# A macaron block on one core: GpSimd multiplies the quantised h by its block scales instead of VectorE, with the order lists rewritten

## The chip, the cores and the metric

The kernel runs on one core of one Trainium2 chip. The metric is the device time of one execution in microseconds (us), smaller is better; the time before is the median of three runs.

## The reference

For 32 sequences of 512 tokens with 256 features the reference computes three residual layers one after the other:

```
x = x + 0.5 * ffn(layernorm(x))        # called A below
x = x + attn(layernorm(x))             # called S: a selective state-space scan, 16 states
x = x + 0.5 * ffn(layernorm(x))        # called C, same weights as A

ffn(x):  gate = q(x) @ q(w_gate).T ; y = q(x) @ q(w_up).T ; h = silu(gate) * y ; return q(h) @ q(w_down).T
q(v):    in blocks of 16: scale = max|v| / 6 ; v / scale rounded to the grid {0, .5, 1, 1.5, 2, 3, 4, 6} ; times scale
attn:    h_t = exp(A dt) h_(t-1) + (...) x_t   for each feature and each of 16 states; y = sum_n h C_n + D x
```

h has 704 features, so each token has 44 blocks of 16, each with a scale.

## The kernel before

All data of a sequence lies with 128 tokens on the partitions, so a sequence has four token tiles (T = 4). An ffn pass quantises x, transposes it, multiplies by the gate and up weights in eight half-tile steps, quantises h tile by tile, transposes h and multiplies by the down weights. The scan has 16 states by 2 halves of the features: 32 steps of 128 x 512.

The engines run a software pipeline. One body of the loop handles one sequence in each of the stages: A (first ffn, pass q = 2 it - 2), S (scan of the sequence before), C (second ffn of the one before that) and N (norm and quantisation of x for the next A). Within a body each engine works through its own list, written out by hand in `ORDER`, strictly in that order; the engines are held together by semaphores alone. 29 bodies use the full lists, and the bodies at either end use the same lists with the stages that exist there. Each piece of a list is a stage, a step and a number. The steps that matter here, with the line of the profile for what they issue:

- ffn, VectorE: `hid` (L717, silu times up, half a tile), `am` (L722, block maxima of a tile of h), `qs` (L728 to L733, scales and their reciprocals for two tiles), `qm` (L737, a maximum with a constant, bf16), `qp` (L743, grid value times block scale into `qh`), `res` (L748, the residual), `xa`, `xs`, `xv`, `xm`, `qy` (L665 to L706, the same quantisation for x), `ln` (L649 to L658).
- ffn, GpSimd: `mv` (L456, h times reciprocal), `mh` (L464 and L471, add and subtract a magic number, which leaves the grid value in `grid`), `mx` (L443, L447, the same for x).
- ffn, ScalarE: `gu` (L939, silu), `ah` and `ax` (L930, L926, absolute value), `ht` (L920, copies transposed h out of PSUM), `tx` (L910).
- ffn, TensorE: `gu` (L1120), `ht` (L1101, transposes `qh`; three to a tile), `dn` (L1127), `tx` (L1082).
- scan, VectorE: `tb`, `cb`, `sc` (L757 to L774), `k` (L786), `dt` (L779, L781), `g` (L793, the scan of one step), `p` (L803, its product with C), `y` (L812).
- scan, GpSimd: `xl` (L426), `bl` (L437). ScalarE: `xh`, `b` (L989), `z` (softplus, L960 to L972), `d` (L999, one decay; exponential). TensorE: `z` (L1160), `k` (L1168), `w` (L1186, the input of one scan step), `c` (L1196), `e` and `p` (L1206).

A scan step m is tied to its neighbours: `g` waits for `w` and `d` of the same m; `w` waits for `g` of m - 2, since it writes the same half of `w_ps`; `w` also needs `b` and `bl` of its state.

## Time and profile before

| what | value |
|---|---|
| time, median of 3 runs (lowest to highest) | 4114.31 us (4113.19 to 4118.74) |
| the profiled execution: time, and its span | 4118.5 us, 4116.8 us |
| mean granted clock of TensorE | 0.970 |
| one body of the steady loop | 122.05 us |

The span runs from the first to the last instruction of the profiled execution. "Busy" is the time in which an engine has an instruction in it. TensorE's ends are modelled, so its busy share is not a share of its peak. The steady bodies repeat each other closely, so one of them (from 2010.2 to 2132.25 us, and its successor) stands for all.

### The profile page before, as it was taken

To read this page: it belongs to the slowest core of one execution; us is meant where nothing else is said; L and a number is where in the kernel's file an instruction comes from. 1 tells how busy PE (TensorE), PEld (TensorE's weight loads), DVE (VectorE), ACT (ScalarE), POOL (GpSimd) and SP (SyncE) were. 2 spreads that over 40 slices of the span, in tenths; PEclk is the share of its full clock that TensorE was granted. 3 is DMA by queue.
4 is the path that set the end of the run, shared out by engine and by line. 5 is a ranking of instruction groups with operands and counts; after the bars stand their busy time and mean duration, and the time that the engine had idled before them with its cause. 6 is when DMAs were issued, how large, how long until landed. Compare 5 with 4: busy or idle time off the path is not lost. (4 is left out here: it accounts for less than half of the span.)

```text
span 4116.8 us, 81697 instructions
## 1 busy us (share of the span) xinstructions
PE 3662.4 (89%) x29740; PEld 2754.3 (67%) x29740; DVE 3740.5 (91%) x6358; ACT 3191.1 (78%) x6115; POOL 2154.0 (52%) x1779
## 2 busy tenths in 40 slices
PE   1689999999999999999999999999999999999986
PEld 0367766667766666776666776666777666677664
DVE  6489999999999999999999999999999999999985
ACT  1368888778888777888877888877788887788863
POOL 1345555555655555555555565555555555556533
PEclk9799999999999999999999999999999999999988
DMA  1000000000000000000000000000000000000000
GB/s 28 11 11 17 7 13 15 17 16 17 6 17 12 17 16 17 17 6 12 16 16 17 17 7 17 11 17 16 17 17 6 12 16 17 17 17 6 11 11 11
DMA packets 46452, 57.93 MB, mean 14 GB/s; under 512 B 7463, under 2 KB 41704, under 8 KB 46056
## 3 DMA queue, kind: packets, MB, share of 16 engines
q1 hardware_dynamic: 46056, 52.72, 3.8%
q8 instruction: 240, 3.93, 0.4%
q14 instruction: 156, 1.28, 0.1%
HBM read 19.16 MB, written 16.78 MB: 9 GB/s over the span
## 5 line engine op out<-in xcount | busy, mean ns | idle before, releaser
L793 DVE TENSOR_TENSOR_SCAN state<-w_ps,decay 128x512 f32<-128x512 f32 x1024 | 1212.9, 1213 | 13.3 <-ACT decay L999 9.2
L1120 PE MATMUL gu_ps<-wgu,qxT 128*128 128x352 f16 x6144 | 1037.0, 319 | 116.7 <-DVE hid L717 78.8
L1120 PEld LDWEIGHTS gu_ps<-wgu,qxT 128*128 128x128 f16 x6144 | 572.6, 99 | 513.1 <-DVE hid L717 126.9
L1186 PE MATMUL w_ps<-bdif,x_parts 128*128 128x129 f16 (+1 forms) x12288 | 866.5, 224 | 46.4 <-DVE state L793 22.8
L1186 PEld LDWEIGHTS w_ps<-bdif,x_parts 128*128 128x128 f16 x12288 | 782.1, 99 | 137.5 <-issue 101.8
L1127 PE MATMUL td_ps<-wd,qhT 128*128 128x256 f32 x3072 | 736.1, 390 | 4.3 <-ACT qhT L920 4.2
L803 DVE SCALAR_TENSOR_TENSOR c_state<-state,inv_A,rep_ps 128x512 f32<-128x512 f32 x1024 | 726.2, 736 | 0.3
L999 ACT ACTIVATE decay<-dt,A_sb 128x512 f32<-128x512 f32 x1024 | 685.2, 718 | 17.7 <-DVE state L793 13.5
L464 POOL TENSOR_TENSOR val<-val,magic 128x704 f32<-128x704 f32 x256 | 408.7, 1597 | 499.3 <-DVE magic L737 499.3
L989 ACT ACTIVATE bdif<-dif,B_tok 128x129 f16<-128x129 f16 x2048 | 642.4, 397 | 18.9 <-DVE B_tok L759 18.9
L1127 PEld LDWEIGHTS td_ps<-wd,qhT 128*128 128x128 f32 x3072 | 570.1, 192 | 90.7 <-issue 14.0
L456 POOL TENSOR_TENSOR val<-hid,recip 128x704 f32<-128x704 f32 x256 | 351.7, 1390 | 531.1 <-DVE recip L733 531.1
L1206 PE MATMUL y_ps<-ident,c_state 128*128 128x128 f32 x4352 | 591.2, 274 | 0.6 <-DVE c_state L803 0.6
L920 ACT COPY qhT<-td_ps 128x256 f32<-128x256 f32 x768 | 282.1, 367 | 361.1 <-PE td_ps L1101 353.1
L437 POOL TENSOR_TENSOR bdif<-dif,B_lo 128x516 f16<-128x516 f16 x512 | 528.0, 1056 | 31.7 <-PE w_ps L1186 31.5
L1206 PEld LDWEIGHTS y_ps<-ident,c_state 128*128 128x128 f32 x4352 | 486.9, 142 | 19.5 <-issue 8.9
L471 POOL TENSOR_TENSOR grid<-val,magic 128x704 f16<-128x704 f32 x256 | 390.8, 1527 | 20.1
L939 ACT ACTIVATE gate<-gu_ps,w_back 128x352 f32<-128x352 f32 x512 | 282.0, 551 | 152.7 <-PE gu_ps L1120 150.1
L1101 PE MATMUL td_ps<-ident,qh 128*128 128x128 f32 x1536 | 308.2, 282 | 93.7 <-issue 42.2
L443 POOL TENSOR_TENSOR x_val<-x_val,x_magic 128x512 f32<-128x512 f32 x128 | 148.4, 1159 | 411.6 <-DVE x_magic L696 411.6
L717 DVE SCALAR_TENSOR_TENSOR hid<-gu_ps,w_back,gate 128x352 f32<-128x352 f32 x512 | 297.1, 580 | 56.6 <-PE gu_ps L1120 43.8
L1101 PEld LDWEIGHTS td_ps<-ident,qh 128*128 128x128 f32 x1536 | 172.8, 141 | 167.3 <-issue 133.6
(143 smaller groups left out, 4366.6 us busy)
## 6 DMA issues: line engine op xcount, KB each, us to landing
x_in<-in_L_attn_x SPq DMA_DIRECT2D x32, 512.0 KB, 3.8
x_s<-x_a SPq DMA_DIRECT2D x32, 512.0 KB, 2.9
out<-x_out SPq DMA_DIRECT2D x32, 512.0 KB, 2.8
hid<-in_L_ffn_w_gate SPq DMA_DIRECT2D x1, 704.0 KB
bdif<-in_L_ffn_w_up SPq DMA_DIRECT2D x1, 704.0 KB
val<-in_L_ffn_w_down SPq DMA_DIRECT2D x1, 704.0 KB, 12.6
W_rBC<-in_L_attn_W_dt SPq DMA_DIRECT2D x1, 64.0 KB
W_dt_sb<-in_L_attn_W_dt SPq DMA_DIRECT2D x1, 64.0 KB
```

Source lines behind the costliest of these rows:

```text
L437: g.tensor_tensor(bdif[:, n % NB, :, 1, 0:P + 1], dif[:, 0:P + 1].unsqueeze(1).broadcast_to([P, T, P + 1]), B_lo[:, :, n:n + 1].broadcast_ ...
L464: g.tensor_tensor(val[:, s], val[:, s], magic[:, s], ALU.add).then_inc(grid_h.sem, 1)
L471: g.tensor_tensor(grid[:, s], val[:, s], magic[:, s], ALU.subtract).then_inc(grid_h.sem, 1)
L793: v.tensor_tensor_scan(state[:, n % 2, gi, :], w_ps[:, gi, :], decay[:, n % 2, gi, :], 0.0, ALU.add, ALU.mult).then_inc(state_ready.sem, 1)
L803: v.scalar_tensor_tensor(c_state[:, n % 2, gi, :], state[:, n % 2, gi, :], inv_A[:, gi, n:n + 1], rep_ps[:], ALU.mult, ALU.mult).then_inc( ...
L989: last = a.activation(bdif[:, n % NB, t, 0, 0:P + 1], dif[:, 0:P + 1], ACT.Copy, scale=B_tok[:, t, n:n + 1])
L999: a.activation(decay[:, n % 2, gi, :], dt[:, gi, :], ACT.Exp, scale=A_sb[:, gi, n:n + 1]).then_inc(decay_ready.sem, 1)
L1101: last = te.transpose(td_ps[:, 0, c * P:(c + 1) * P], qh[:, t, (part * 2 + c) * P:(part * 2 + c + 1) * P], ident[:])
L1120: last = te.matmul(gu_ps[:, m, 0:FH], qxT[:, t // 2, 4 * (t % 2) + xp * G + c], wgu[:, c, wp, a:a + FH], start=begin, stop=end)
L1127: last = te.matmul(td_ps[:, 1, :], qhT[:, t % 2, c], wd[:, c, :], start=c == 0, stop=c == FC - 1)
L1186: last = te.matmul(w_ps[:, gi, t * P:t * P + wide], x_parts[:, xp, t, gi * P:(gi + 1) * P], bdif[:, n % NB, t, bp, 0:wide], start=(t, xp, ...
L1206: last = te.matmul(y_ps[:, t // 2, col:col + P], c_state[:, n % 2, gi, t * P:(t + 1) * P], ident[:], is_transpose=True, start=(j, t % 2) = ...
```

## The change

Step `qp` leaves VectorE's list and enters GpSimd's, eight times a body. The operands, the element count (128 x 704) and the result tile stay. x's own product (`qy`) stays on VectorE. Since `scale` is now read by GpSimd, `scales_h` gets a wait for the products of the pass before. All four lists are reordered.

```diff
--- before.py
+++ after.py
@@ -26,39 +26,38 @@
 
 ORDER = {
     "PE": """
-    A.gu0 A.gu1 A.gu2 S.xt0 A.gu3 S.rb0 S.bt0 A.gu4 A.gu5 S.z0 S.k0 S.k1 S.w0 S.w1 S.c0 A.gu6 A.gu7 A.ht0 S.e0
-    S.e1 A.ht1 A.ht2 S.w2 S.w3 A.dn0 S.c1 S.w4 C.tx0 S.p0 A.ht3 S.p1 S.p2 A.ht4 S.w5 A.ht5 S.c2 C.tx1 A.dn1 S.w6
-    S.p3 S.w7 S.c3 C.gu0 S.w8 S.w9 S.p4 S.p5 S.c4 C.gu1 S.p6 C.gu2 A.ht6 S.w10 S.w11 S.c5 C.gu3 S.p7 S.w12 S.p8
-    S.p9 S.p10 A.ht7 S.c6 C.gu4 A.ht8 S.w13 S.w14 A.dn2 S.w15 C.gu5 S.c7 A.ht9 S.p11 S.w16 S.w17 A.ht10 S.c8
-    C.gu6 S.p12 S.p13 S.p14 S.p15 A.ht11 S.w18 S.w19 C.gu7 S.c9 A.dn3 S.w20 S.p16 S.w21 S.c10 C.ht0 S.p17 C.ht1
-    S.p18 S.p19 C.ht2 S.w22 C.dn0 S.w23 S.w24 C.ht3 S.c11 S.p20 S.p21 C.ht4 S.w25 S.p22 C.ht5 S.w26 C.dn1 S.c12
-    S.w27 C.ht6 S.w28 C.ht7 S.p23 S.c13 C.ht8 S.w29 C.dn2 S.p24 S.p25 C.ht9 S.p26 S.p27 C.ht10 S.c14 S.w30
-    C.ht11 S.w31 S.p28 S.c15 C.dn3 N.tx0 S.p29 N.tx1 S.p30 S.p31
+    A.gu0 A.gu1 A.gu2 S.xt0 A.gu3 S.rb0 S.bt0 A.gu4 A.gu5 S.z0 A.gu6 S.k0 S.k1 S.w0 S.e0 S.w1 S.c0 A.gu7 S.e1
+    A.ht0 A.ht1 C.tx0 S.w2 A.ht2 S.w3 A.dn0 S.c1 S.p0 S.w4 A.ht3 S.p1 S.p2 A.ht4 S.w5 S.c2 A.ht5 C.tx1 S.p3
+    A.dn1 S.w6 S.w7 S.p4 S.c3 C.gu0 S.p5 S.w8 S.w9 S.c4 C.gu1 S.w10 A.ht6 C.gu2 S.w11 A.ht7 C.gu3 S.p6 S.c5
+    A.ht8 S.p7 S.w12 S.p8 S.p9 S.w13 S.c6 C.gu4 A.dn2 S.w14 S.w15 C.gu5 S.c7 S.p10 A.ht9 S.p11 S.w16 S.w17 C.gu6
+    S.c8 A.ht10 S.p12 S.p13 S.p14 S.w18 S.w19 A.ht11 S.c9 C.gu7 S.p15 A.dn3 S.w20 S.w21 C.ht0 S.p16 S.c10 C.ht1
+    S.p17 S.p18 C.ht2 S.w22 S.w23 C.dn0 S.w24 S.c11 S.p19 S.p20 C.ht3 S.p21 S.p22 C.ht4 S.w25 S.c12 C.ht5 S.w26
+    C.dn1 S.w27 C.ht6 S.p23 S.p24 C.ht7 S.w28 S.c13 C.ht8 S.w29 C.dn2 S.c14 S.p25 C.ht9 S.p26 S.p27 C.ht10 S.w30
+    C.ht11 S.w31 C.dn3 N.tx0 S.c15 N.tx1 S.p28 S.p29 S.p30 S.p31
     """,
     "DVE": """
-    S.ln0 A.hid0 C.ln0 A.hid1 A.am0 A.hid2 C.xa0 C.xa1 C.xs0 C.xv0 C.xv1 C.xm0 A.hid3 A.am1 S.cb0 S.tb0 A.qs0
-    A.hid4 S.sc0 S.k0 S.k1 A.qm0 A.hid5 C.xm1 A.am2 S.dt0 A.hid6 A.qp0 C.qy0 A.qm1 S.g0 S.g1 S.p0 S.p1 S.g2 S.g3
-    A.hid7 A.res0 A.qp1 S.p2 A.am3 S.p3 C.qy1 A.qs1 S.g4 S.g5 S.p4 S.p5 S.g6 S.g7 S.p6 A.qm2 S.p7 S.g8 C.hid0
-    S.g9 A.res1 A.qp2 A.qm3 C.hid1 S.p8 S.p9 C.am0 C.hid2 S.g10 S.g11 S.p10 S.p11 C.hid3 S.g12 C.am1 S.p12 A.qp3
-    C.qs0 S.g13 S.g14 S.p13 C.hid4 C.qm0 A.res2 S.g15 C.hid5 S.p14 S.p15 C.am2 C.qm1 C.qp0 S.g16 S.g17 S.p16
-    S.p17 C.hid6 S.g18 S.g19 C.hid7 S.p18 C.am3 S.p19 C.qs1 A.res3 S.g20 S.g21 S.p20 C.qp1 N.ln0 C.qm2 S.g22
-    S.p21 C.res0 S.g23 S.p22 S.g24 S.g25 S.p23 C.qp2 C.qm3 S.g26 C.res1 N.xa0 N.xa1 S.p24 S.p25 S.g27 N.xs0
-    N.xv0 N.xv1 C.qp3 S.p26 S.p27 N.xm0 N.xm1 C.res2 S.g28 S.g29 S.p28 S.p29 S.g30 S.g31 N.qy0 N.qy1 S.p30 S.p31
-    C.res3 S.y0
+    S.ln0 A.hid0 C.ln0 A.hid1 A.am0 A.hid2 C.xa0 C.xa1 C.xs0 C.xv0 C.xv1 C.xm0 A.hid3 S.tb0 A.am1 A.qs0 A.hid4
+    S.sc0 S.cb0 A.qm0 A.hid5 A.am2 S.k0 S.k1 S.dt0 A.hid6 C.xm1 C.qy0 A.qm1 A.hid7 S.g0 S.g1 S.p0 S.p1 S.g2 S.g3
+    A.res0 S.p2 S.p3 A.am3 C.qy1 A.qs1 S.g4 S.g5 S.p4 S.p5 S.g6 A.qm2 A.qm3 S.g7 S.p6 S.p7 A.res1 C.hid0 S.g8
+    S.g9 C.hid1 S.p8 S.p9 C.am0 C.hid2 S.g10 S.g11 S.p10 C.hid3 S.p11 C.am1 S.g12 C.qs0 S.g13 S.p12 S.p13 A.res2
+    C.hid4 S.g14 S.g15 C.qm0 C.qm1 C.hid5 S.p14 S.p15 C.am2 S.g16 S.g17 S.p16 S.p17 C.hid6 S.g18 S.g19 S.p18
+    C.hid7 S.p19 C.am3 C.qs1 A.res3 S.g20 S.g21 N.ln0 C.qm2 S.g22 S.p20 S.p21 S.g23 C.res0 S.p22 S.p23 S.g24
+    N.xa0 N.xa1 C.qm3 S.g25 S.g26 S.p24 C.res1 S.p25 S.g27 N.xs0 N.xv0 S.p26 N.xv1 S.p27 N.xm0 N.xm1 C.res2
+    S.g28 S.g29 S.p28 S.p29 S.g30 N.qy0 N.qy1 S.g31 S.p30 S.p31 C.res3 S.y0
     """,
     "ACT": """
-    A.gu0 A.gu1 S.ln0 A.gu2 C.ln0 S.xt0 A.gu3 S.xh0 C.ax0 S.rb0 C.ax1 A.gu4 S.b0 S.b1 A.gu5 A.ah0 S.z0 A.gu6
-    A.ah1 S.d0 A.ht0 S.d1 A.ht1 S.b2 A.ht2 S.d2 S.d3 A.gu7 S.d4 S.d5 A.ht3 S.d6 A.ht4 A.ht5 S.b3 S.b4 C.tx0
-    A.ah2 C.tx1 S.d7 S.d8 S.d9 S.d10 C.gu0 S.b5 A.ah3 C.gu1 S.b6 S.b7 C.gu2 S.d11 S.d12 A.ht6 C.gu3 S.d13 S.d14
-    A.ht7 S.b8 A.ht8 S.d15 S.d16 C.gu4 C.ah0 C.ah1 C.gu5 S.b9 A.ht9 S.d17 S.d18 S.d19 A.ht10 C.gu6 S.b10 A.ht11
-    C.gu7 S.d20 S.d21 S.d22 S.d23 S.b11 C.ht0 C.ht1 C.ht2 C.ah2 S.b12 S.b13 S.d24 S.d25 S.d26 C.ht3 S.d27 C.ht4
-    C.ht5 C.ah3 S.b14 N.ln0 C.ht6 C.ht7 C.ht8 S.d28 S.d29 S.b15 S.d30 N.ax0 N.ax1 C.ht9 S.d31 C.ht10 C.ht11
+    A.gu0 A.gu1 S.ln0 A.gu2 C.ln0 S.xt0 A.gu3 C.ax0 S.rb0 S.xh0 S.b0 A.gu4 S.b1 A.ah0 A.gu5 S.z0 A.gu6 C.ax1
+    A.ah1 A.gu7 S.d0 A.ht0 S.d1 S.d2 A.ht1 A.ht2 S.d3 S.d4 S.b2 S.b3 S.b4 A.ht3 A.ht4 S.d5 A.ht5 C.tx0 C.tx1
+    S.d6 A.ah2 A.ah3 S.d7 S.d8 S.d9 S.d10 C.gu0 S.b5 S.b6 C.gu1 S.b7 A.ht6 C.gu2 S.d11 A.ht7 C.gu3 S.d12 S.d13
+    S.d14 A.ht8 S.d15 C.gu4 S.b8 S.b9 C.ah0 C.ah1 C.gu5 S.d16 S.d17 S.d18 S.d19 A.ht9 C.gu6 A.ht10 S.b10 S.b11
+    C.gu7 A.ht11 S.b12 S.d20 S.d21 S.d22 S.d23 C.ht0 C.ht1 C.ht2 C.ah2 C.ah3 S.b13 S.d24 S.d25 S.d26 N.ln0 C.ht3
+    C.ht4 C.ht5 S.b14 S.b15 S.d27 S.d28 S.d29 C.ht6 S.d30 C.ht7 C.ht8 N.ax0 S.d31 N.ax1 C.ht9 C.ht10 C.ht11
     N.tx0 N.tx1
     """,
     "POOL": """
-    S.ln0 C.ln0 C.mx0 A.mv0 A.mv1 S.xl0 S.bl0 S.bl1 A.mh0 A.mh1 S.bl2 S.bl3 C.mx1 A.mv2 A.mv3 S.bl4 S.bl5 S.bl6
-    A.mh2 A.mh3 S.bl7 S.bl8 S.bl9 C.mv0 C.mv1 C.mh0 C.mh1 S.bl10 S.bl11 S.bl12 S.bl13 C.mv2 S.bl14 C.mh2 C.mv3
-    N.ln0 C.mh3 S.bl15 N.mx0 N.mx1
+    S.ln0 C.ln0 C.mx0 A.mv0 A.mv1 A.mh0 S.xl0 S.bl0 S.bl1 A.qp0 A.mh1 S.bl2 A.qp1 S.bl3 C.mx1 A.mv2 A.mv3 S.bl4
+    S.bl5 A.mh2 A.qp2 S.bl6 A.mh3 S.bl7 S.bl8 S.bl9 S.bl10 C.mv0 C.mv1 A.qp3 S.bl11 C.mh0 C.qp0 C.mh1 C.qp1
+    S.bl12 S.bl13 C.mv2 C.mv3 S.bl14 N.ln0 C.mh2 S.bl15 C.qp2 C.mh3 C.qp3 N.mx0 N.mx1
     """,
 }
 
@@ -470,6 +469,15 @@
                         pool.wait_ge(qh_ready.sem, qh_ready.at(q - 1, T - 1 + t))
                 g.tensor_tensor(grid[:, s], val[:, s], magic[:, s], ALU.subtract).then_inc(grid_h.sem, 1)
 
+            def quantised_h(q, t):
+                if not first(q):
+                    pool.wait_ge(tr_full.sem, tr_full.at(q - 1, HP * t + HP))
+                pool.wait_ge(grid_h.sem, grid_h.at(q, 2 * t + 2))
+                g.tensor_tensor(qh[:, t, 0:F].rearrange("p (b i) -> p b i", i=BLOCK),
+                                grid[:, t % 2].rearrange("p (b i) -> p b i", i=BLOCK),
+                                scale[:, t * HB:(t + 1) * HB].unsqueeze(2).broadcast_to([P, HB, BLOCK]),
+                                ALU.mult).then_inc(qh_ready.sem, 1)
+
             def body(it, pieces, pass_a, pass_c, pass_n):
                 unit = {"A": pass_a, "C": pass_c, "N": pass_n, "S": it - 1}
                 for stage, step, k in pieces:
@@ -487,6 +495,8 @@
                         values_h(unit[stage], k)
                     elif step == "mh":
                         round_h(unit[stage], k)
+                    elif step == "qp":
+                        quantised_h(unit[stage], k)
 
             body(-1, order("POOL", "N"), None, None, 0)
             body(0, order("POOL", "AN"), 0, None, 1)
@@ -725,6 +735,8 @@
             def scales_h(q, half):
                 s = slice(2 * half * HB, (2 * half + 2) * HB)
                 dve.wait_ge(qh_step.sem, qh_step.at(q, 5 * half + 2))
+                if not first(q):
+                    dve.wait_ge(qh_ready.sem, qh_ready.at(q - 1, 2 * half + 2))
                 v.tensor_scalar(scale[:, s], amax[:, s], 1.0 / 6.0, MIN_SCALE, ALU.mult,
                                 ALU.max).then_inc(qh_step.sem, 1)
                 dve.wait_ge(qh_step.sem, qh_step.at(q, 5 * half + 3))
@@ -735,13 +747,6 @@
             def magic_h(q, t):
                 dve.wait_ge(abs_ready.sem, abs_ready.at(q, t + 1))
                 v.tensor_scalar(magic[:, t % 2], magic[:, t % 2], MAGIC, None, ALU.max).then_inc(magic_ready.sem, 1)
-
-            def quantised_h(q, t):
-                if not first(q):
-                    dve.wait_ge(tr_full.sem, tr_full.at(q - 1, HP * t + HP))
-                dve.wait_ge(grid_h.sem, grid_h.at(q, 2 * t + 2))
-                v.tensor_tensor(by_block(qh[:, t, 0:F], HB), by_block(grid[:, t % 2], HB),
-                                per_block(scale[:, t * HB:(t + 1) * HB]), ALU.mult).then_inc(qh_ready.sem, 1)
 
             def ffn_residual(q, t, src, dst):
                 dve.wait_ge(dn_ready.sem, dn_ready.at(q, t + 1))
@@ -862,8 +867,6 @@
                         scales_h(q[stage], k)
                     elif step == "qm":
                         magic_h(q[stage], k)
-                    elif step == "qp":
-                        quantised_h(q[stage], k)
                     elif step == "res":
                         if stage == "C" and k == 0:
                             if not first(it - 2):
```

## Rows read from the trace of the kernel before

**Rows 1.** The page, busy time of each engine: us, share of the span, instructions.

```profile
PE 3662.4 (89%) x29740; PEld 2754.3 (67%) x29740; DVE 3740.5 (91%) x6358; ACT 3191.1 (78%) x6115; POOL 2154.0 (52%) x1779
```

**Rows 2.** Windows, one body of the steady loop: engines, granted clock, DMA.

```profile
core 0: us, PE busy (x) PEld busy (x) DVE busy (x) ACT busy (x) POOL busy (x), PEclk, DMA share, GB/s
2010.20:2132.25 122.05, 113.59 (x929) 85.73 (x928) 114.84 (x197) 99.86 (x192) 66.97 (x56) 0.97 0.04 14
```

**Rows 3.** Timeline of VectorE, parts of one body.

```profile
2010.19 0.69 DVE L786 TENSOR_TENSOR c_state<-xT,w_ps 128x512 f32<-128x512 f32 x1 [2.55 <-PE w_ps L1168]
...
2018.84 0.88 DVE L743 TENSOR_TENSOR qh<-grid,scale 128x704 f32<-128x704 f16 x1
2019.64 0.42 DVE L706 TENSOR_TENSOR qx<-x_grid,x_scale_hi 128x512 f16<-128x512 f16 x1
...
2020.57 2.33 DVE L793 TENSOR_TENSOR_SCAN state<-w_ps,decay 128x512 f32<-128x512 f32 x2
...
2027.31 1.68 DVE L743 TENSOR_TENSOR qh<-grid,scale 128x704 f32<-128x704 f16 x1
...
2111.45 1.40 DVE L649 BATCH_NORM_STATS2 s_stats<-x_a 128x6 f32<-128x256 f32 x4
...
2132.25 0.69 DVE L786 TENSOR_TENSOR c_state<-xT,w_ps 128x512 f32<-128x512 f32 x1 [2.55 <-PE w_ps L1168]
...
2142.59 2.34 DVE L793 TENSOR_TENSOR_SCAN state<-w_ps,decay 128x512 f32<-128x512 f32 x2 [0.32 <-ACT decay L999]
```

**Rows 4.** Groups of VectorE: the product of h and the steps beside it.

```profile
L743 DVE TENSOR_TENSOR qh<-grid,scale 128x704 f32<-128x704 f16 x256 | 243.2, 950 | 10.1 <-POOL grid L471 10.0
...
L737 DVE TENSOR_SCALAR magic<-magic 128x704 bf16<-128x704 bf16 x256 | 109.6, 428 | 9.2 <-ACT magic L930 9.0
```

**Rows 5.** Windows: end of the head, and the scan stretch of one body.

```profile
2133.00:2144.20 11.20, 8.95 (x64) 6.41 (x64) 10.08 (x14) 11.06 (x17) 6.41 (x6) 0.85 0.01 1
2144.20:2232.00 87.80, 85.05 (x772) 69.22 (x771) 86.18 (x135) 71.23 (x143) 50.60 (x41) 1.00 0.02 7
```

**Rows 6.** Timeline of TensorE around the first differences and transposes.

```profile
2133.85 2.75 PE L1186 MATMUL w_ps<-bdif,x_parts 128*128 128x129 f16 x24 [0.78 <-DVE c_state L786]
...
2143.98 0.41 PE L1101 MATMUL td_ps<-ident,qh 128*128 128x128 f32 x2 [0.61 <-ACT qhT L920]
2144.22 1.70 PE L1186 MATMUL w_ps<-bdif,x_parts 128*128 128x129 f16 x24
...
2222.40 0.41 PE L1101 MATMUL td_ps<-ident,qh 128*128 128x128 f32 x2 [1.37 <-issue]
```

**Rows 7.** Timeline of ScalarE, from the last softplus step to the first decay.

```profile
2014.76 1.15 ACT L972 ACTIVATE soft<-soft 128x512 f32<-128x512 f32 x2
2015.93 1.28 ACT L939 ACT_TABLE_LOAD   x1
2017.23 0.56 ACT L939 ACTIVATE gate<-gu_ps,w_back 128x352 f32<-128x352 f32 x1
2017.68 0.78 ACT L930 ACTIVATE magic<-val 128x704 bf16<-128x704 f32 x1
2018.48 1.28 ACT L999 ACT_TABLE_LOAD   x1
2019.78 0.72 ACT L999 ACTIVATE decay<-dt,A_sb 128x512 f32<-128x512 f32 x1
...
2123.74 0.62 ACT L926 ACTIVATE x_magic<-x_val 128x512 bf16<-128x512 f32 x1
```

**Rows 8.** Groups of GpSimd on a tile of h.

```profile
L464 POOL TENSOR_TENSOR val<-val,magic 128x704 f32<-128x704 f32 x256 | 408.7, 1597 | 499.3 <-DVE magic L737 499.3
L471 POOL TENSOR_TENSOR grid<-val,magic 128x704 f16<-128x704 f32 x256 | 390.8, 1527 | 20.1
L456 POOL TENSOR_TENSOR val<-hid,recip 128x704 f32<-128x704 f32 x256 | 351.7, 1390 | 531.1 <-DVE recip L733 531.1
```

**Rows 9.** Timeline of GpSimd while the product of 2027.31 us waited.

```profile
2027.08 1.16 POOL L447 TENSOR_TENSOR x_grid<-x_val,x_magic 128x512 f16<-128x512 f32 x1
```

## The prediction

> **What bounds the kernel now.** The page first, for the busy shares [rows 1]: VectorE 91%, TensorE 89%, ScalarE 78%, GpSimd 52%. The lead of VectorE is small, so the next view is one body by windows [rows 2]. In 122.05 us VectorE is busy 114.84 us and TensorE 113.59 us. The place of the same instruction in two bodies (2010.19 and 2132.25 us) gives the period: 122.06 us [rows 3]. With 29 full bodies and one nearly full one, what a body gains counts 30 times.
>
> A body has two parts with different limits. The **head** runs from the layer norm of S at 2111.45 us to the first scan at 2142.59 us, 31.1 us [rows 3]. There VectorE waits for products of other engines; the 2.55 us before 2010.19 is the largest such wait. A latency chain through all engines sets its length: norm, transposes, projections, softplus, dt, first decay. The **scan stretch** is the rest. In its window from 2144.20 to 2232.00 TensorE is busy 85.05 us of 87.80 and VectorE 86.18 us, at a granted clock of 1.00, the upper level of 2.4 GHz [rows 5]. The reader is to see that both are nearly full in the same stretch, not in turns. VectorE sets the pace (its timeline there shows hardly an idle bracket), but TensorE stands only 87.80 - 85.05 = 2.75 us behind it, 1.37 us of it in one wait before a transpose of `qh` [rows 6].
>
> **What is removed.** Eight products a body. One is 950 ns in the mean [rows 4], 243.2 us in all, or 7.6 us a body. Back to back it takes less: from 2018.84 to the next start at 2019.64 is 0.80 us [rows 3], so at least 8 x 0.80 = 6.4 us. If VectorE alone set the end, a body would lose 6.4 to 7.6 us. One of the eight (A.qp0) lies in the head, seven in the scan stretch: 7 x 0.80 = 5.6 us there. That would leave VectorE some 86.2 - 5.6 = 80.6 us of work against TensorE's 85.05 us. So after the first 2.75 us TensorE becomes the bound, and the remainder turns into idle time of VectorE. This is the step on which the forecast rests. The change takes nothing from TensorE: the list has the same 140 pieces.
>
> How much of the 2.75 us goes? TensorE still has to wait here and there: for ScalarE's copies of h (0.61 us at 2143.98 [rows 6]), for scans. Bounds: all of it stays, or none. In the new lists VectorE's pieces lie behind TensorE's by a few us almost everywhere in the stretch (C.res2 and w20 for instance have to wait for TensorE, not the reverse), so I take 0.7 us as what stays: a gain of 2.05 us.
>
> **What is added on GpSimd.** Eight products. The nearest row is L456, the same shape with the same broadcast of a block factor, at 1390 ns; the other steps on a tile of h take 1527 and 1597 ns [rows 8]. I take 1.39, between 1.39 and 1.60: 8 x 1.39 = 11.1 us a body, 12.8 at most. GpSimd's 66.97 us [rows 2] become some 78 of 120, so it is no bound by its sum. What counts is lateness: TensorE's `ht` is in order, and whatever is behind it waits too. Following the new lists with the durations above, each `qp` ends 3 us or more before its transpose comes up (A.qp1, for instance, has only mh1 and bl2 ahead of it, while its `ht3` on TensorE stands behind two `w`, the whole of dn0, c1, p0 and w4). I cost this at nothing; with that cover gone each product is 1.39 - 0.80 = 0.6 us later for TensorE, 4.7 us a body. The new wait in `scales_h` is on products of the previous pass, tens of us old: nothing; behind it on VectorE stand the reciprocal, and for that GpSimd's `mv`.
>
> **The port.** At 2027.31 the product took 1.68 us instead of 0.88 [rows 3], while GpSimd was on L447 from 2027.08 to 2028.24 [rows 9]; 2028.24 + 0.88 = 2029.1 is about where it ended (2028.99). So VectorE's instruction stood until GpSimd's was through. For the product the mean, 0.95, less 0.88 makes 0.07, or 0.56 us for the eight of a body; `qm`, also between two SBUF tiles, may pay as much [rows 4]. With GpSimd's busy share up from 55% to 65%, I expect such stalls to grow by a fifth, well under 1 us a body with the stall of the product itself gone, and they fall on VectorE, which now has time to spare. Nothing in the sum; 1 us if VectorE were still the bound. The Trainium skill, SBUF — State Buffer, section Who interferes with whom, says the same of the mechanism: a VectorE instruction with two SBUF inputs, or in a 2-port mode, and a GpSimd instruction that reads SBUF exclude each other for the whole instruction. The Trainium skill, Perfetto Trace Analysis, section Optimizing Scalar/DVE Operations, speaks against the change: moving work between these two "might not help", because they share that port. By it the 7.6 us would come back as stalls and the time would not fall; by the row, a stall needs an overlap with one of the few kinds of instruction that share it, and scans and C products, the bulk, show none.
>
> **What the lists move.** ScalarE: I counted the changes between silu and exponential along each list: 15 table loads a body before, 13 after. Each is 1.28 us [rows 7], so 2.6 us less on an engine that is not the bound: nothing by itself, though it helps the copies of h to come in time.
>
> The head is where the lists cost. Before, ScalarE goes from the last softplus step (ends 2015.91) through a table load, silu 6, `ah1`, a load and the first decay to the scan at 2020.57: 4.66 us [rows 7, 3]. After, `ax1` (0.62 us) and silu 7 (0.56 us) stand before that decay as well: +1.2 us. Silu 7 needs A.gu7 on TensorE, which now stands behind gu6, k, w0, e0, w1 and c0, and w0 waits longer, since on GpSimd the 3.1 us of A.mh0 now precede the low parts of x and B. TensorE idles before w0 as before (0.78 us at 2133.85), where the granted clock over 2133.0 to 2144.2 was 0.85 [rows 5, 6]: its two `w` took 2.75 us instead of 1.70 at 2144.22, that is, part of the stretch was at the lower level of 1.2 GHz. In the chain above, silu 7 is then just ready or up to 1 us late. First scan: +1.2 us, from 0 (if earlier `ah0` and `cb` shorten softplus's start) to +3. TensorE's w2 has to follow the end of the first scan, which it did before with 0.5 us to spare (2143.8, start at 2144.22), and its remaining list from w2 on is as long as before. So the stretch begins +0.9 us later.
>
> **The sum.** Per body -2.05 + 0.9 = -1.15 us; 30 bodies: -34.5 us. At both ends of the program single passes run alone, and a product is then on the chain at 1.39 instead of 0.88 us: some six of them count, +3 us. Total -31.5 us. Against the profiled execution, 4118.5 - 31.5 = 4087.0 us; that execution was 4.2 us above the median, so against the median 4114.3 - 31.5 = **4083 us**, 0.8% faster. Its own range, with the idle time left and the head within the bounds above, not both at one end: 4035 to 4106.
>
> **The rivals.**
> - *VectorE is the only bound* (TensorE's busy time is modelled and hides slack): 6.4 to 7.6 us a body, 7.0 in the middle, less 1 us of port stalls and 1 of the head: -5 x 30 = -150, with the ends 3967 us. For it: VectorE has no idle in the stretch. Against: TensorE's 85.05 of 87.80 us, and its groups start at the same spacing wherever they recur. A halfway case, 2 us of hidden slack more, gives 4083 - 60 = 4023. Together 0.14.
> - *No change* (4106 to 4122 us, say 4114): head and stretch cancel, idle of TensorE stays near 2 us. 0.15.
> - *The head decides, slower*: the first scan starts later by the price of silu 7 waiting for gu7, which waits for w0, which waits for GpSimd's mh0. With A.mh0's 3.1 us fully on the chain, +3.0 - 2.05 = +0.95 us a body, 28.5 us in 30, with the ends 4146 us. It decides from a first scan 2.2 us later on (2.05, and 8 us / 30 for what can be told, less the ends). For it: mh0, xl0, bl0 are 6.2 us in a row. Against: softplus on ScalarE runs beside them. 0.16.
> - *The port eats the gain*, as the skill's page has it: VectorE stays the bound and stalls 5.6 us more in the stretch; 4114 plus the head's 27 and the ends' 3, 4144 us; 0.02, within slower.
>
> **The numbers.** Forecast 0.53 (4035 to 4106), larger gain 0.14, no change 0.15, slower 0.18. What a measurement of this kernel can tell from no change is about 0.2%, 8.2 us. Faster 0.67, same 0.15, slower 0.18. The range takes the forecast, half of the larger gain and the lower part of slower: 4020 to 4128.
>
> **What would show it.** In the changed profile: VectorE busy some 107 us a body and idle in brackets behind `w` and `td_ps`; TensorE as busy as before per body and 95% or more of the stretch; 13 table loads; GpSimd near 78 us; the product on GpSimd at about 1.39 us; the first scan 32.4 us after the norm of S instead of 31.1; period near 120.9 us. Wrong if the period falls below 119 (TensorE had hidden slack) or the first scan starts more than 2.2 us later.

## The result, and the profile after

| | before | after |
|---|---|---|
| time, median of 6 runs (lowest to highest) | 4114.09 us (4110.94 to 4118.74) | 4096.85 us (4093.64 to 4101.27) |
| ratio, 95% interval | | 0.9959 (0.9947 to 0.9971) |
| profiled execution: time, span | 4118.5, 4116.8 us | 4099.19, 4097.2 us |
| mean granted clock | 0.970 | 0.969 |

The change makes the kernel 17 us faster, 0.4%. The forecast was 31 us, 0.8%.

The page after, busy time of each engine (beside [rows 1]):

```profile
PE 3644.5 (89%) x29740; PEld 2769.3 (68%) x29740; DVE 3531.7 (86%) x6102; ACT 3108.4 (76%) x6053; POOL 2482.3 (61%) x2035
```

VectorE lost 208.8 us of busy time, 6.5 us for each of the 32 sequences, and is no longer ahead. TensorE is. The time fell by only a twelfth of the 208.8 us.

Windows after: one body, between two instructions that begin `k`; and the scan stretch behind its head (beside [rows 2, 5], whose columns they have):

```profile
1999.88:2121.49 121.61, 112.92 (x929) 86.07 (x928) 108.08 (x189) 97.17 (x190) 77.31 (x64) 0.97 0.04 14
...
2133.30:2220.30 87.00, 86.10 (x780) 70.58 (x778) 82.41 (x131) 69.80 (x142) 57.96 (x47) 1.00 0.04 14
```

In the stretch TensorE is busy 86.10 of 87.00 us, 99%, and VectorE 82.41, 95%. Before, the idle time was 2.75 us on TensorE and 1.62 on VectorE; now it is 0.90 and 4.59. The two have changed places.

Groups of VectorE after (beside [rows 4]): the scan, its product with C, `qm`, the two residuals and the dt product.

```profile
L798 DVE TENSOR_TENSOR_SCAN state<-w_ps,decay 128x512 f32<-128x512 f32 x1024 | 1212.0, 1211 | 59.3 <-ACT decay L1002 39.2 <-PE w_ps L1189 19.5 <-issue 0.2
L808 DVE SCALAR_TENSOR_TENSOR c_state<-state,inv_A,rep_ps 128x512 f32<-128x512 f32 x1024 | 722.3, 737 | 35.3 <-PE rep_ps L1199 18.3 <-PE y_ps L1209 14.5 <-issue 2.1
L749 DVE TENSOR_SCALAR magic<-magic 128x704 bf16<-128x704 bf16 x256 | 84.9, 352 | 14.4 <-ACT magic L933 13.4
L784 DVE TENSOR_TENSOR dt<-dt,soft 128x1024 f32<-128x1024 f32 x32 | 66.0, 2062 | 72.5 <-ACT soft L975 72.5
L753 DVE SCALAR_TENSOR_TENSOR x_a<-td_ps,x_in 128x256 f32<-128x256 f32 x128 | 53.9, 421 | 40.2 <-PE td_ps L1130 40.2
L753 DVE SCALAR_TENSOR_TENSOR x_out<-td_ps,x_c 128x256 f32<-128x256 f32 x128 | 53.3, 417 | 29.8 <-PE td_ps L1130 29.8
```

The last column is where VectorE's freed time went. It now waits for TensorE before residuals (70.0 us in the two groups, 36.0 before) and before `p` (35.3 us, 0.3 before), and before scans for decays and `w` (59.3 us, 13.3 before).

Groups of GpSimd after (beside [rows 8]), the product last:

```profile
L463 POOL TENSOR_TENSOR val<-val,magic 128x704 f32<-128x704 f32 x256 | 392.0, 1531 | 214.8 <-DVE magic L749 214.8
L470 POOL TENSOR_TENSOR grid<-val,magic 128x704 f16<-128x704 f32 x256 | 390.5, 1525 | 20.1
L476 POOL TENSOR_TENSOR qh<-grid,scale 128x704 f32<-128x704 f16 x256 | 354.6, 1385 | 19.0 <-POOL grid L470 0.4
```

Now the head. First GpSimd, then TensorE (with one window, columns as above), ScalarE and VectorE, in timelines after (beside [rows 3, 6, 7]); the layer norm of S of this body starts at 2098.71 us.

```profile
2117.78 1.52 POOL L463 TENSOR_TENSOR val<-val,magic 128x704 f32<-128x704 f32 x1 [0.43 <-DVE magic L749]
2119.37 1.52 POOL L470 TENSOR_TENSOR grid<-val,magic 128x704 f16<-128x704 f32 x1
2120.85 2.14 POOL L425 TENSOR_TENSOR x_parts<-s_xh,x_parts 128x1024 f16<-128x1024 f32 x1
2122.93 2.07 POOL L436 TENSOR_TENSOR bdif<-dif,B_lo 128x516 f16<-128x516 f16 x2
2124.95 1.40 POOL L476 TENSOR_TENSOR qh<-grid,scale 128x704 f32<-128x704 f16 x1
```

```profile
2124.25 1.46 PE L1189 MATMUL w_ps<-bdif,x_parts 128*128 128x129 f16 x12 [1.95 <-POOL bdif L436]
2125.50 1.06 PE L1209 MATMUL y_ps<-ident,c_state 128*128 128x128 f32 x4
2126.36 1.42 PE L1189 MATMUL w_ps<-bdif,x_parts 128*128 128x129 f16 x12
2127.71 0.39 PE L1199 MATMUL rep_ps<-C_parts,pick_row 48*128 48x512 f16 x1
2128.03 1.96 PE L1123 MATMUL gu_ps<-wgu,qxT 128*128 128x352 f16 x12
...
2133.13 0.84 PE L1189 MATMUL w_ps<-bdif,x_parts 128*128 128x129 f16 x12
```

```profile
2124.20:2128.00 3.80, 3.75 (x29) 3.40 (x29) 2.63 (x2) 3.77 (x6) 2.14 (x2) 0.56 0.02 4
```

```profile
2127.07 0.62 ACT L929 ACTIVATE x_magic<-x_val 128x512 bf16<-128x512 f32 x1
2127.59 0.78 ACT L933 ACTIVATE magic<-val 128x704 bf16<-128x704 f32 x1
2129.14 0.55 ACT L942 ACTIVATE gate<-gu_ps,w_back 128x352 f32<-128x352 f32 x1 [0.77 <-PE gu_ps L1123]
2129.71 1.28 ACT L1002 ACT_TABLE_LOAD   x1
2131.00 0.72 ACT L1002 ACTIVATE decay<-dt,A_sb 128x512 f32<-128x512 f32 x1
```

```profile
2121.49 0.69 DVE L791 TENSOR_TENSOR c_state<-xT,w_ps 128x512 f32<-128x512 f32 x1 [2.25 <-PE w_ps L1171]
...
2125.34 2.09 DVE L784 TENSOR_TENSOR dt<-dt,soft 128x1024 f32<-128x1024 f32 x1 [2.31 <-ACT soft L975]
...
2131.76 2.34 DVE L798 TENSOR_TENSOR_SCAN state<-w_ps,decay 128x512 f32<-128x512 f32 x2 [1.14 <-ACT decay L1002]
```

Read it from the top. `A.mh0` (two instructions from 2117.78) now stands ahead of the low parts of x and B. So B's part for `w0` comes late, and TensorE waits 1.95 us for it (the bracket at 2124.25; 0.78 us in [rows 6]). After that wait `w0` and `w1` take 1.46 and 1.42 us, against 0.84 for the same twelve matmuls at 2133.13: over 2124.2 to 2128.0 the granted clock is 0.56, so most of it at the lower level of 1.2 GHz. Over the whole run `w` waits 60.4 us for this part, 31 times, 1.95 us each. `gu7` starts at 2128.03, silu 7 waits 0.77 us for it, and the table load and the first decay stand behind silu 7.

One body is a sample. For 29 bodies in a row the starts of the S norm and of the first scan after it were taken from VectorE's timeline, and the differences averaged. "Head" is norm to first scan, "stretch" is first scan to next norm. The 29 run from the second full body to the one behind the last full one, which has no N; over the 29 full bodies themselves every stretch is 0.07 to 0.16 us longer, and the gain of 2.77 us below is 2.83. The table has them for all kernels that ran, in us:

| kernel | head | stretch | body |
|---|---|---|---|
| before | 31.15 | 90.42 | 121.57 |
| after | 33.32 | 87.65 | 120.97 |
| `low_first` | 32.32 | 87.73 | 120.06 |
| `move_alone` | 31.16 | 90.20 | 121.35 |
| `te_less_before` | 31.13 | 89.87 | 121.01 |
| `te_less_after` | 32.96 | 85.64 | 118.59 |
| `lists_alone` | 32.95 | 97.89 | 130.84 |
| `lists_alone2` | 33.04 | 94.81 | 127.84 |
| `gate7_late` | 31.76 | 91.02 | 122.78 |
| `one_load_less` | 32.38 | 88.88 | 121.27 |
| `act_less_before` | 31.14 | 90.19 | 121.33 |
| `act_less_after` | 33.42 | 87.63 | 121.04 |
| `act_less_move` | 31.17 | 89.61 | 120.78 |
| `qp0_after_dt` | 33.35 | 87.63 | 120.97 |

The change takes 2.77 us from the stretch and puts 2.17 us into the head. That leaves 0.60 us a body, 17.4 us in 29, of the 19.6 us between the two profiled spans. Such an average is as good as the execution that it comes from, and single executions scatter by a few us: the profiled one of before lies 4.4 us above its median and that of after 2.3, that of `move_alone` 4.1 below. That is 0.15 us a body, so differences of that size in the table say nothing.

### The profile page after: what moved, and what is told of

Same layout as the page of the kernel before. It is cut to its first block and busy times, and to the rows that moved or that the text cites. A ratio compares the mean times of both kernels' runs of the same rounds, so it can differ in the third digit from the quotient of the medians.

```text
span 4097.2 us, 81761 instructions
## 1 busy us (share of the span) xinstructions
PE 3644.5 (89%) x29740; PEld 2769.3 (68%) x29740; DVE 3531.7 (86%) x6102; ACT 3108.4 (76%) x6053; POOL 2482.3 (61%) x2035
## 5 line engine op out<-in xcount | busy, mean ns | idle before, releaser
L798 DVE TENSOR_TENSOR_SCAN state<-w_ps,decay 128x512 f32<-128x512 f32 x1024 | 1212.0, 1211 | 59.3 <-ACT decay L1002 39.2
L1123 PE MATMUL gu_ps<-wgu,qxT 128*128 128x352 f16 x6144 | 1021.0, 317 | 89.1 <-DVE hid L727 61.5
L1189 PE MATMUL w_ps<-bdif,x_parts 128*128 128x129 f16 (+1 forms) x12288 | 865.5, 224 | 82.3 <-POOL bdif L436 60.4
L1189 PEld LDWEIGHTS w_ps<-bdif,x_parts 128*128 128x128 f16 x12288 | 790.6, 100 | 163.9 <-issue 130.5
L808 DVE SCALAR_TENSOR_TENSOR c_state<-state,inv_A,rep_ps 128x512 f32<-128x512 f32 x1024 | 722.3, 737 | 35.3 <-PE rep_ps L1199 18.3
L992 ACT ACTIVATE bdif<-dif,B_tok 128x129 f16<-128x129 f16 x2048 | 633.9, 396 | 8.4 <-DVE B_tok L764 8.2
L1209 PE MATMUL y_ps<-ident,c_state 128*128 128x128 f32 x4352 | 616.0, 280 | 0.6 <-DVE c_state L808 0.4
L455 POOL TENSOR_TENSOR val<-hid,recip 128x704 f32<-128x704 f32 x256 | 349.7, 1387 | 318.9 <-DVE recip L745 318.9
L1209 PEld LDWEIGHTS y_ps<-ident,c_state 128*128 128x128 f32 x4352 | 499.7, 144 | 40.6 <-issue 31.1
L463 POOL TENSOR_TENSOR val<-val,magic 128x704 f32<-128x704 f32 x256 | 392.0, 1531 | 214.8 <-DVE magic L749 214.8
L1104 PE MATMUL td_ps<-ident,qh 128*128 128x128 f32 x1536 | 310.2, 284 | 72.0 <-ACT qhT L923 56.9
L476 POOL TENSOR_TENSOR qh<-grid,scale 128x704 f32<-128x704 f16 x256 | 354.6, 1385 | 19.0 <-POOL grid L470 0.4
```

The source lines that it names most:

```text
L463: g.tensor_tensor(val[:, s], val[:, s], magic[:, s], ALU.add).then_inc(grid_h.sem, 1)
L476: g.tensor_tensor(qh[:, t, 0:F].rearrange("p (b i) -> p b i", i=BLOCK), grid[:, t % 2].rearrange("p (b i) -> p b i", i=BLOCK), scale[:, t ...
L798: v.tensor_tensor_scan(state[:, n % 2, gi, :], w_ps[:, gi, :], decay[:, n % 2, gi, :], 0.0, ALU.add, ALU.mult).then_inc(state_ready.sem, 1)
L808: v.scalar_tensor_tensor(c_state[:, n % 2, gi, :], state[:, n % 2, gi, :], inv_A[:, gi, n:n + 1], rep_ps[:], ALU.mult, ALU.mult).then_inc( ...
L992: last = a.activation(bdif[:, n % NB, t, 0, 0:P + 1], dif[:, 0:P + 1], ACT.Copy, scale=B_tok[:, t, n:n + 1])
L1123: last = te.matmul(gu_ps[:, m, 0:FH], qxT[:, t // 2, 4 * (t % 2) + xp * G + c], wgu[:, c, wp, a:a + FH], start=begin, stop=end)
```

## The experiments

Differences in us are taken between a kernel's median and that of the kernel before, run beside it on the same chip. The change itself stands at -17.2.

| kernel | median, us | kernel before, beside it | ratio, 95% interval |
|---|---|---|---|
| `move_alone` | 4114.13 | 4110.75 | 1.0009 (1.0000 to 1.0018) |
| `lists_alone` | 4410.03 | 4110.75 | 1.0730 (1.0716 to 1.0745) |
| `qp0_after_dt` | 4099.63 | 4110.75 | 0.9973 (0.9962 to 0.9984) |
| `low_first` | 4069.76 | 4110.75 | 0.9902 (0.9888 to 0.9915) |
| `te_less_before` | 4097.43 | 4114.94 | 0.9963 (0.9949 to 0.9976) |
| `te_less_after` | 4024.96 | 4114.94 | 0.9785 (0.9771 to 0.9799) |
| `lists_alone2` | 4312.89 | 4114.94 | 1.0481 (1.0467 to 1.0496) |
| `gate7_late` | 4157.77 | 4114.94 | 1.0105 (1.0091 to 1.0118) |
| `act_less_before` | 4108.68 | 4112.05 | 0.9993 (0.9984 to 1.0002) |
| `act_less_after` | 4097.88 | 4112.05 | 0.9970 (0.9959 to 0.9982) |
| `act_less_move` | 4095.02 | 4112.05 | 0.9961 (0.9948 to 0.9973) |
| `one_load_less` | 4109.82 | 4112.05 | 0.9999 (0.9990 to 1.0008) |

### The move without the new lists

`move_alone` has the changed code with the old lists: the `qp` are struck from VectorE's list, and on GpSimd each follows its own `mh`.

```diff
 "POOL":
-    ... S.bl1 A.mh0 A.mh1 S.bl2 S.bl3 C.mx1 ... A.mh2 A.mh3 S.bl7 ... C.mh0 C.mh1 S.bl10 ... C.mh2 C.mv3 N.ln0 C.mh3 S.bl15 ...
+    ... S.bl1 A.mh0 A.qp0 A.mh1 A.qp1 S.bl2 S.bl3 C.mx1 ... A.mh2 A.qp2 A.mh3 A.qp3 S.bl7 ... C.mh0 C.qp0 C.mh1 C.qp1
+    S.bl10 ... C.mh2 C.qp2 C.mv3 N.ln0 C.mh3 C.qp3 S.bl15 ...
```

> The eight products of a body go to GpSimd, each directly behind its mh, and every other piece keeps the order of the kernel before. Theory 1 (in the scan stretch TensorE takes over as the bound after some 2 us, and what the changed kernel lost again it lost in the head, through the new lists): the head stays at 31.1 us, the stretch falls from 90.95 to about 88.9 us, body about 120.0, time 4114 - 60 = 4054 us (4040 to 4075). Theory 2 (the lists are what makes the move pay; with the old order the products come late on GpSimd and hold the transposes of TensorE): 4105 us or more.

It gains nothing: +3.4 us. The expected 4054 is wrong by 60 us, and the other theory is right that the move by itself is worth nothing, but not in its reason, that the products would come late on GpSimd and hold TensorE's transposes: TensorE waits for the product 8.9 us in the whole run, against 11.6 us before. The head is the old one (31.16 us), and the stretch is less by 0.22 us, little more than the scatter named above. One stretch in windows, then the groups of VectorE that grew, then TensorE's waits in that stretch, all of `move_alone`:

```profile
2015.50:2104.50 89.00, 86.40 (x784) 70.59 (x782) 83.51 (x128) 72.68 (x147) 61.48 (x49) 1.00 0.02 7
```

```profile
L748 DVE TENSOR_SCALAR magic<-magic 128x704 bf16<-128x704 bf16 x256 | 142.4, 556 | 20.5 <-ACT magic L932 17.2
L785 DVE TENSOR_SCALAR dt<-dt 128x1024 f32<-128x1024 f32 x32 | 55.0, 1718 | 1.1
```

```profile
2017.55 0.41 PE L1103 MATMUL td_ps<-ident,qh 128*128 128x128 f32 x2 [0.61 <-ACT qhT L922]
...
2089.05 0.39 PE L1198 MATMUL rep_ps<-C_parts,pick_row 48*128 48x512 f16 x1 [0.45 <-DVE c_state L807]
2090.27 0.84 PE L1188 MATMUL w_ps<-bdif,x_parts 128*128 128x129 f16 x12 [0.47 <-DVE state L797]
2095.21 0.41 PE L1103 MATMUL td_ps<-ident,qh 128*128 128x128 f32 x2 [0.57 <-issue]
```

VectorE is idle 5.5 of 89 us, and still TensorE is idle 2.6. One bracket of TensorE shrank, the one before a transpose of `qh` (1.37 us in [rows 6], 0.57 here; such waits without a releaser are 42.2 us in the run before and 19.6 in this one). Others grew: its gate and up products wait 103.8 us in the run for `hid`, against 78.8. VectorE in turn waits 67.3 us before scans, against 13.3. So with more room on VectorE TensorE's idle time moves to other pieces of the list and hardly falls. Stalls at the port cost VectorE another 2 us a body (`qm` 556 ns against 428, the clip of dt 1718 ns against 720).

### The new lists without the move

`lists_alone` and `lists_alone2` have the new order on all engines, and the product on VectorE. Where it stands in that list had to be chosen. The two differ in that choice alone; the later positions of the second:

```diff
 "DVE" (lists_alone2, against the changed kernel):
-    A.hid6 C.xm1 ... S.p1 S.g2 ... C.hid1 S.p8 ... S.p13 A.res2 ... S.g17 S.p16 ... C.qs1 A.res3 ... S.g24 N.xa0 ... S.p26 N.xv1
+    A.hid6 A.qp0 C.xm1 ... S.p1 A.qp1 S.g2 ... C.hid1 A.qp2 S.p8 ... S.p13 A.qp3 A.res2 ... S.g17 C.qp0 S.p16 ...
+    C.qs1 C.qp1 A.res3 ... S.g24 C.qp2 N.xa0 ... S.p26 C.qp3 N.xv1
```

> The lists of the changed kernel, but with the product left on VectorE, each piece at its old neighbours. Theory 1: VectorE is the bound of the stretch again (about 91 us) and the head is 1 to 2 us longer, body 123 to 124, time 4135 to 4175 us, middle 4155. Theory 2 (the new lists carry the gain by themselves): 4114 us or less.

> The new lists with the product on VectorE once more, each piece now where its grid was ready in the trace of the changed kernel (in the first attempt VectorE waited 112 us in all for GpSimd's grid). Theory 1: without those waits VectorE bounds the stretch again at 90 to 92 us, the head is 2 us longer than before, body 123 to 125, time 4140 to 4200 us, middle 4165. Theory 2 (the new lists carry the gain by themselves): 4114 us or less.

The first came out at +299 us, with this group of VectorE:

```profile
L741 DVE TENSOR_TENSOR qh<-grid,scale 128x704 f32<-128x704 f16 x256 | 325.9, 1273 | 112.3 <-POOL grid L469 112.3
```

The 112.3 us are waits for the grid values: the product stood too early, so the size says something about the chosen positions. The second has it later, and that wait is gone:

```profile
L741 DVE TENSOR_TENSOR qh<-grid,scale 128x704 f32<-128x704 f16 x256 | 324.2, 1266 | 8.7 <-POOL grid L469 8.4 <-issue 0.2
```

It is still +198 us, against an expectation of 4140 to 4200. The product itself is 316 ns longer than before, 2.5 us a body, since it now coincides with work of GpSimd. So in neither of the two placements does the new order alone make the kernel faster, which was the rival theory. Its price with the product on VectorE stays open, since hand-placed positions are in it.

### Which engine a body hangs on

`te_less_before` and `te_less_after` leave out the third of the three partial products of gate and up in stage C, in the kernel before and in the changed one. That was reckoned at 4.8 us of TensorE a body; TensorE's busy time fell by 116.3 us before and 137.0 after, 3.6 and 4.3 us for each sequence.

```diff
-                        gate_up(q[stage], k)
+                        gate_up(q[stage], k, PARTS[:2] if stage == "C" else PARTS)
```

> The kernel before, with the third of the three partial products (low part of x by high part of the weights) left out of the gate and up products of stage C alone: 8 x 4 fewer matmuls of 352 columns a body at 0.15 us each, 4.8 us less work for TensorE, all of it in the scan stretch. Theory 1 (VectorE sets the pace of the stretch before the change): hardly faster, 0 to 0.5 us a body, 4095 to 4112 us, middle 4104. Theory 4 (TensorE bounded the stretch already): 4114 less at least 2.5 x 30, below 4040.

> The same 4.8 us of TensorE's work left out of the changed kernel. Theory 1 (TensorE has become the bound of the stretch: busy 86.1 of 87.0 us, VectorE 82.4): the stretch shrinks to what VectorE needs, 3 to 4.5 us a body, 90 to 135 us in all, 3965 to 4010, middle 3985. Rival (stalls at the port or waits on ScalarE keep the stretch where it is): less than 25 us, above 4072.

Before, the edit is worth 0.56 us a body (121.57 to 121.01), 17.5 us in all. After, it is worth 2.38 us a body (120.97 to 118.59), and the time goes from -17.2 to -90.0. So the body hangs on TensorE some four times as much after the change (3.5 times for each us by which its busy time fell). It came less far than expected (3965 to 4010), and the window of `te_less_after` shows how far it got:

```profile
2102.60:2184.20 81.60, 78.77 (x718) 64.88 (x718) 78.69 (x125) 67.99 (x140) 57.16 (x46) 1.00 0.03 8
```

With TensorE lightened, both engines are at 96.5%, and neither fills the stretch. TensorE's waits for ScalarE's copies of h grew from 56.9 to 88.2 us in the run; the time is 40 us above the middle of the expected range. That the order of the pieces sets these waits is argued, not shown.

`act_less_before`, `act_less_after` and `act_less_move` leave out half of ScalarE's copies of B for 12 of the 16 states, reckoned at 7.2 us of ScalarE a body, in the kernel before, the changed one and `move_alone`. ScalarE's busy time fell by 214, 216 and 210 us, 6.6 to 6.7 us for each sequence.

```diff
-                for t in range(T):
+                for t in range(T if n < NB else T // 2):
```

> The kernel before, with half of ScalarE's copies of B (two of four, for states 4 to 15) left out: 24 x 0.30 = 7.2 us less work for ScalarE a body. Theory 1 (VectorE sets the pace of the stretch): no or hardly any gain, 4095 to 4114 us, middle 4106. Theory 5 (ScalarE, 97% busy from 40 us to 80 us of a body, already bounded the first half of the stretch): below 4085.

> The same in the changed kernel. Theory 1 (TensorE bounds the stretch at 99% busy): at most the 1 us of TensorE that is left idle, 4070 to 4097 us, middle 4085. Theory 5 (ScalarE is the bound after the change): below 4060.

> The same in move_alone, which gained nothing although VectorE had 4.7 us a body less to do. Theory 5 (with VectorE relieved and the old order, ScalarE with its 15 table loads is what holds that kernel): the gain of the move appears, 4114 - 60 = 4054 us or less. Theory 6 (the old order itself holds it: TensorE's pieces stand behind VectorE's and ScalarE's whatever these cost): no more than in the kernel before, 4095 to 4114 us.

In the first two nothing follows: 0.9993 before, an interval that holds 1, and 0.9970 against 0.9959 after, intervals that overlap. ScalarE's sum is not on the path of either. In `move_alone` it frees 20 us (+3.4 to -17.0), a third of what 4054 asked for. So ScalarE explains a part of what holds `move_alone`. For the larger part the order is what is left, the 2 us of stalls a body on VectorE included; no run shows which pairs of pieces, or which of the four lists, hold the kernel.

### The head

`low_first` is the changed kernel with one piece of GpSimd's list, `A.mh0`, put back behind the three short ones that `w0` needs:

```diff
 "POOL":
-    ... A.mv0 A.mv1 A.mh0 S.xl0 S.bl0 S.bl1 A.qp0 A.mh1 ...
+    ... A.mv0 A.mv1 S.xl0 S.bl0 S.bl1 A.mh0 A.qp0 A.mh1 ...
```

> The changed kernel with one move on GpSimd: the low parts of x and B (xl0, bl0, bl1) before A.mh0, as in the kernel before. Theory 1 (w0 waits 1.95 us for them, gu7 stands behind w0, silu 7 waits 0.77 us for gu7, and the first decay for silu 7): the first scan comes 0.77 us earlier, 23 us in 30 bodies, 4074 us (4068 to 4085). Theory 3 (the port stall at dt sets the first scan): the stall stays, and so does the time, 4097 us within 6.

It is the fastest of all, -41.0 us, and its interval (0.9888 to 0.9915) lies clear of the change's (0.9947 to 0.9971). The head is 1.00 us shorter than the changed kernel's, and the stretch is the same within 0.08 us. Its timelines of TensorE (with one window) and ScalarE, the norm of S being at 2085.39:

```profile
2109.99 0.84 PE L1188 MATMUL w_ps<-bdif,x_parts 128*128 128x129 f16 x12
2110.67 0.60 PE L1208 MATMUL y_ps<-ident,c_state 128*128 128x128 f32 x4
2111.11 0.85 PE L1188 MATMUL w_ps<-bdif,x_parts 128*128 128x129 f16 x12
...
2113.92 1.07 PE L1122 MATMUL gu_ps<-wgu,qxT 128*128 128x352 f16 x6 [1.65 <-ACT gate L941]
```

```profile
2109.90:2112.30 2.40, 2.36 (x30) 1.91 (x29) 0.96 (x2) 2.37 (x4) 2.26 (x2) 1.00 0.04 10
```

```profile
2115.03 0.55 ACT L941 ACTIVATE gate<-gu_ps,w_back 128x352 f32<-128x352 f32 x1
2115.60 1.28 ACT L1001 ACT_TABLE_LOAD   x1
2116.89 0.72 ACT L1001 ACTIVATE decay<-dt,A_sb 128x512 f32<-128x512 f32 x1
```

`w0` does not wait, it takes 0.84 us (granted clock 1.00 over 2109.9 to 2112.3), and silu 7 has no bracket. What is left between softplus and the first decay is a run of instructions on ScalarE without a bracket, and `gu7` now waits for silu 6. Softplus ends 26.5 us after the norm in the kernel before, 26.6 in the changed one and 26.6 here, so the differences of the head lie behind it.

`qp0_after_dt` is the changed kernel in which GpSimd waits for dt before `A.qp0`, so that it cannot stand in the way of VectorE's dt product.

```diff
+                        if stage == "A" and k == 0 and pass_a is not None and not (isinstance(it, int) and it == 0):
+                            pool.wait_ge(dt_ready.sem, dt_ready.at(unit["S"], 1))
```

> The changed kernel with one more wait: GpSimd begins A.qp0 only when dt is done, so that this product can't hold up VectorE's two-input add of dt, which took 2.06 us instead of 1.23. Theory 1 (the first decay waits for silu 7 and its table load, and dt is ready 2.9 us before it): no change, 4097 us within 6. Theory 3 (the stall at the shared port stands on the chain of the head): the add is back at 1.23 us and the time falls by 0.84 x 30 = 25 us, to 4072.

The group of the dt product in `qp0_after_dt`:

```profile
L786 DVE TENSOR_TENSOR dt<-dt,soft 128x1024 f32<-128x1024 f32 x32 | 39.2, 1225 | 72.6 <-ACT soft L977 72.6
```

The stall is gone there (2062 to 1225 ns) and the time is that of the changed kernel (0.9973 against 0.9959, overlapping; head 33.35 against 33.32). A part of it comes back at `xm` (302 to 440 ns, 17.7 of the 26.8 us), but dt is ready 0.8 us earlier and the first scan is not. So the stall is real and off the path: the first decay has to wait for silu 7 anyway.

### Two attempts to better `low_first`

`gate7_late` moves silu 7 behind four decays, with what belongs to it on the other engines, to take its 0.56 us off the head. ScalarE has one more pair of table loads by that. `one_load_less` moves one decay behind a silu, so that one pair falls away.

```diff
 gate7_late, "ACT":
-    ... A.ah1 A.gu7 S.d0 A.ht0 S.d1 S.d2 A.ht1 A.ht2 S.d3 S.d4 ...
+    ... A.ah1 S.d0 A.ht0 S.d1 S.d2 A.ht1 A.ht2 S.d3 A.gu7 S.d4 ...
 gate7_late, "DVE":
-    ... A.qm1 A.hid7 S.g0 S.g1 S.p0 S.p1 S.g2 S.g3 A.res0 ...
+    ... A.qm1 S.g0 S.g1 S.p0 S.p1 S.g2 S.g3 A.hid7 A.res0 ...
 gate7_late, "PE":
-    ... A.ht0 A.ht1 C.tx0 S.w2 A.ht2 S.w3 A.dn0 S.c1 S.p0 S.w4 A.ht3 ...
+    ... A.ht0 A.ht1 S.w2 A.ht2 S.w3 A.dn0 S.c1 S.p0 S.w4 C.tx0 A.ht3 ...
 one_load_less, "ACT":
-    ... C.gu2 S.d11 A.ht7 C.gu3 S.d12 ...
+    ... C.gu2 A.ht7 C.gu3 S.d11 S.d12 ...
```

> low_first with the end of the head as in the kernel before: silu 7 on ScalarE behind the first four decays (two table loads more), hid7 on VectorE behind g3, C.tx0 on TensorE behind w4. Theory 1 (what stands between softplus and the first decay sets the first scan): 0.55 us earlier, and the stretch as it was, 4070 - 17 = 4053 us (4045 to 4062). Rival (ScalarE's two extra loads, 2.6 us a body, come back as late copies of h in a stretch where TensorE can't wait): 4070 us or more.

> low_first with one decay (d11) moved behind silu 3 of stage C on ScalarE, so that one pair of table loads a body goes, 2.57 us less for ScalarE. gate7_late had one pair more and lost 88 us. Theory 1 (TensorE bounds the stretch, and ScalarE's load matters only where it comes late): 4070 us within 8. Theory 5 (ScalarE's sum matters throughout): 4000 to 4050 us.

`gate7_late` loses 84 us against `low_first` (+42.8 and -41.0): its head is shorter by the 0.56 us, its stretch longer by 3.29. `one_load_less` loses 39 us (-2.2 and -41.0), though ScalarE has 1.28 us x 2 less to do in each body. Neither theory had the second. For `gate7_late` the rival's figure, 4070 us or more, is met. The scan's group in `low_first`, in `gate7_late` and in `one_load_less`:

```profile
L797 DVE TENSOR_TENSOR_SCAN state<-w_ps,decay 128x512 f32<-128x512 f32 x1024 | 1210.7, 1209 | 47.2 <-ACT decay L1001 27.1 <-PE w_ps L1188 19.4 <-issue 0.2
```

```profile
L797 DVE TENSOR_TENSOR_SCAN state<-w_ps,decay 128x512 f32<-128x512 f32 x1024 | 1217.0, 1213 | 149.0 <-ACT decay L1001 84.9 <-PE w_ps L1188 63.5 <-issue 0.2
```

```profile
L797 DVE TENSOR_TENSOR_SCAN state<-w_ps,decay 128x512 f32<-128x512 f32 x1024 | 1214.4, 1212 | 129.4 <-ACT decay L1001 109.3 <-PE w_ps L1188 19.5 <-issue 0.2
```

The waits for decays grow by 58 and by 82 us, and in `gate7_late` those for `w` by 44. Three rows show where from: TensorE's wait in `gate7_late`, and the late scan in `one_load_less` with the silu ahead of its decay.

```profile
2171.73 0.86 PE L1188 MATMUL w_ps<-bdif,x_parts 128*128 128x129 f16 x12 [1.85 <-ACT bdif L991]
```

```profile
2161.95 1.22 DVE L797 TENSOR_TENSOR_SCAN state<-w_ps,decay 128x512 f32<-128x512 f32 x1 [2.65 <-ACT decay L1001]
```

```profile
2159.32 0.55 ACT L941 ACTIVATE gate<-gu_ps,w_back 128x352 f32<-128x352 f32 x1 [0.47 <-PE gu_ps L1122]
```

In `gate7_late` ScalarE's copies of B come late behind the extra pair of loads: `w` waits 56.1 us for them in the run, 31 times, a wait that `low_first` does not have. So for this part of the loss the rival had the mechanism, with copies of B in place of those of h. In `one_load_less` d11 now stands behind silu 3, which stands behind a copy of h and its own product of TensorE; it begins 4.56 us after silu 2 of stage C, against 1.86 us in `low_first`. One decay or one copy of B that comes late stops the scan, whatever ScalarE's sum is.

## Why the prediction was right, and where it was off

**What becomes the bound.** Right. The prediction had TensorE take over after 2.75 us, with 0.7 us of idle left; TensorE is idle 0.90 us of the stretch in the window. The gain in the stretch was to be 2.05 us, and, as the stretch is cut here, another 0.3 because it begins 1.2 us later by the first scan and 0.9 by `w2`, 2.35 together. It is 2.77. VectorE as the only bound would have taken 5.6 us or more out of it. The `te_less` pair confirms it by intervention: TensorE's work is worth four times as much after.

**But not for the reason given.** The prediction took the gain as following from the removal, and the new lists as bystanders there. `move_alone` shows that the removal with the old lists gives at most 0.22 us a body in the stretch, and nothing in time. `lists_alone` and `lists_alone2` show that the lists without the removal do not give it either, in the two placements of the product that ran. The gain came with both together. The step that failed is the silent one in "so after the first 2.75 us TensorE becomes the bound": it assumes that TensorE's idle time came from VectorE being full. In `move_alone` VectorE is idle 5.5 of 89 us and TensorE still 2.6. What in the new lists lets TensorE close up is not shown, so that the stretch came out near its figure is in part luck.

**The head.** This is the term that was mis-sized. It was +1.2 us, for `ax1` and silu 7 before the first decay, with silu 7 "just ready or up to 1 us late", taken as just ready. Measured is +2.17. `low_first` splits it: with `A.mh0` behind the parts for `w0` the head is +1.17 us, the predicted 1.2, and the other 1.00 us comes of `A.mh0` ahead of the parts that `w0` needs: the wait, and the slower matmuls behind it. The prediction named that chain, had its rows, and bounded it rightly at 1 us. It took the wrong end. In 29 bodies that is 29 us; the whole forecast gain was 31.

**The sum.** -2.77 + 2.17 = -0.60 us a body, 18 us in 30, against -1.15 and 34.5. The direction is right and the size about half, 17 us against 31. The errors have opposite signs: the stretch gave 0.4 more, the head took 1.0 more. The ends were to cost 3 us; with 18 of the 19.6 us in the bodies, they gave 1.6. The mechanism of the slower rival was half at work, since `w0` did wait, 1.95 us, for parts that stand behind `mh0`; it moved the first scan by 1.0 us in place of 3.0. It was said to decide from a first scan 2.2 us later; at 2.17 it came close, and the kernel stayed faster through the larger gain in the stretch.

**The product on GpSimd.** Right: 1385 ns against 1.39 us, GpSimd at 77.31 us a body against 78. Its lateness was put at nothing, and so it is: TensorE's transposes wait 4.1 us for it in the whole run, against 11.6 us before.

**The port.** Nothing in the sum, and so it is, though by another route than "stalls grow by a fifth". The dt product stalls 0.83 us (26.5 us in all), `qs` and the copy of B another 15 us, while `qm` and `xm` lose 24.7 and 31.5 us of stalls (428 to 352 ns, 547 to 302 ns). The sum goes down by some 15 us. The prediction had not named dt. `qp0_after_dt` shows that the stall of dt costs nothing there.

**The loads.** 13 table loads a body, as counted: the four groups of ScalarE have 406 in 31 bodies, against 468. By itself that is worth nothing, as forecast, with the `act_less` pair as the evidence: 6.7 us off ScalarE move neither kernel. `one_load_less` adds what the prediction did not have: where the loads lie can cost 1.2 us a body.

**The wait in `scales_h`.** Nothing, as predicted: the step before the reciprocal shows 2.3 us of idle in its whole group, in the changed kernel and in `low_first` alike.

**VectorE's own figures.** 107 us a body were expected, the window shows 108.08. The brackets lie behind `td_ps` and `rep_ps` as said, and more of them behind decays (39.2 us) than behind `w` (19.5 us), which was not.

## What to carry to other kernels

Before work is taken from the busiest engine, look at the second engine's idle time in the same stretch, and at each bracket of it: what it waits for decides whether relief reaches it. Here the same move was worth nothing (3 us slower, at the edge of what can be told) or 17 us, by the order around it. When work goes to an engine with its own fixed order, look for the short pieces that others wait for, and keep them ahead of the long ones; one long piece in front of three short ones cost 24 us here, more than the change gained. And an engine that is off the path by its sum can be on it by one late result: judge it by who waits for its pieces, not by its busy share.

## What the hardware showed that was not expected

- A stall at the port between VectorE and GpSimd falls on whichever of a few kinds of VectorE's instructions stands there, and moves with the order. The scan (1212 ns) and its product with C (737 ns) show none. The dt product takes 1225 ns alone and 2062 ns beside `A.qp0`; the clip of dt, with one fp32 input in SBUF, 694 ns and 1718 ns; the bf16 maximum `qm` 352 to 579 ns in the mean, and 2.28 us in one place of `low_first`; the product of h 950 and 1266 ns. `low_first` has 57 us more of `qm` than the changed kernel and is the faster one.
- GpSimd makes the product of 704 elements in 1385 ns, VectorE in 0.88 us without a stall: a factor of 1.57, though GpSimd's three other steps on the same tile take no less, 1387 to 1531 ns in the mean. With `move_alone`'s order the same product takes 1495 ns.
- A wait of TensorE can cost more than itself. After 1.95 us of waiting, `w0`, `e0` and `w1` took 1.46, 1.06 and 1.42 us, against 0.84, 0.60 and 0.85 in `low_first`, where it did not wait there: 1.65 us more for the same work, at a granted clock of 0.56 against 1.00. The kernel before has the same at its `w0` and `w1`, 0.50 over 2133.8 to 2136.6, after a wait of 0.78 us. But not every wait does that: in `low_first` `gu7` begins after 1.65 us of waiting, at 2113.92, and the granted clock over 2113.9 to 2116.2 is 1.00; in the changed kernel it is 1.00 over 2132.1 to 2134.0, after a wait of 1.48 us. So the length of the wait alone does not decide it, and no run here shows what does. The mean granted clock of the whole run goes with it: 0.970, 0.969, and 0.978 in `low_first`.
